# One core, a state-space mixer and a sparse FFN: base rows moved to VectorE, packed attention, and an earlier token choice

## What is computed

```python
h  = layernorm(x) * (1 + ca) + sa
x  = x + ga * mixer(h)            # x, z projections, causal conv, silu, B, C, dt, state scan,
                                  # group norm, gate by silu(z), output projection
h  = layernorm(x) * (1 + cb) + sb
x  = x + gb * ffn(h)

def ffn(h):
    weights = h @ router_w + router_b
    idx     = sorted indices of the 127 largest weights      # of 1024 tokens
    xs      = h[idx]
    q, k, v = heads(rmsnorm(xs) @ wq, wk, wv)                # 16 heads of 16, rope on q and k
    a       = softmax(q @ k.T / 4 + mask[idx, idx])
    x1      = xs + (a @ v) @ wo
    x2      = x1 + gelu(rmsnorm(x1) @ w1) @ w2
    out     = 0; out[idx] = x2 * weights[idx]
    return out + h * (1 - (weights > threshold))
```

## Time and profile before

| what | value |
|---|---|
| runs | 1646.09, 1646.8, 1646.9 us; median 1646.8 |
| profiled execution | 1651.24 us |
| its span | 1649.5 us, 23125 instructions |
| mean granted TensorE clock | 0.942 of 2.4 GHz |
| busy: VectorE | 990.2 us (60%) |
| busy: ScalarE | 688.7 us (42%) |
| busy: GpSimd | 482.9 us (29%) |
| chain that ended last | TensorE 76%, VectorE 11%, issue 4%, ScalarE 3%, DMA 2%, GpSimd 2% |

### The profile page before, as it was taken

How to read it: one execution, slowest core, us unless ns; L and a number is a source line. 1 busy time by engine, 2 the same in 40 slices (tenths; PEclk the granted TensorE clock), 3 DMA queues, 4 the chain that set the end, 5 groups by cost and what they waited for, 6 DMA issues and landing times.

```text
span 1649.5 us, 23125 instructions
## 1 busy us (share of the span) xinstructions
PE 1455.1 (88%) x8673; PEld 931.3 (56%) x8736; DVE 990.2 (60%) x2632; ACT 688.7 (42%) x1345; POOL 482.9 (29%) x505
## 2 busy tenths in 40 slices
PE   7999989989799897999989997998979989897445
PEld 2447545765467654675447654675546754466434
DVE  2337675368735695376763787356862669537661
ACT  4443533436244452635435362444516354252221
POOL 3014231322505323133313325043231432323240
PEclk9999999999999999999999999899999999999666
DMA  8000000100102000020000101020010200001010
GB/s 274 1 1 27 26 29 13 43 27 26 42 1 69 7 33 29 1 69 26 28 15 26 44 26 42 0 68 1 32 36 1 69 20 20 29 4 40 26 42 4
DMA packets 47534, 54.25 MB, mean 33 GB/s; under 512 B 7608, under 2 KB 42296, under 8 KB 47424
## 3 DMA queue, kind: packets, MB, share of 16 engines
q1 hardware_dynamic: 41408, 46.42, 8.6%
q0 software_dynamic: 6016, 6.35, 1.5%
HBM read 34.84 MB, written 17.87 MB: 32 GB/s over the span
## 4 chain that ended last, share of the span: by engine, by line
PE 76%; DVE 11%; issue 4%; ACT 3%; DMA 2%; POOL 2%; POOLq 0%; DVEq 0%; SPq 0%
PE ps L1515 36%; PE ps L1679 7%; PE ps L1630 4%; PE ps L1589 3%; PE ps L1582 3%; DMA Mt<-mask,midx 2%; PE ps L1642 2%; PE ps L1601 2%; PE ps L1816 2%; PE ps L1826 2%; DVE xT L1199 2%; PE ps L1794 2%; PE ps L1616 2%; PE ps L1620 1%; PE ps L1607 1%
## 5 line engine op out<-in xcount | busy, mean ns | idle before, releaser
L1515 PE MATMUL ps<-xT,wc_s 128*128 128x512 f32 x512 | 235.8, 608 | 0.0
L1515 PE MATMUL ps<-xT,wb_s 128*128 128x512 f32 x512 | 235.1, 608 | 0.1
L1022 DVE SCALAR_TENSOR_TENSOR xT<-xc,cols_s,xT 128x512 f32<-128x512 f32 x192 | 168.4, 923 | 3.2 <-ACT xT L713 0.6
L1515 PEld LDWEIGHTS ps<-xT,wb_s 128*128 128x128 f32 x512 | 97.2, 196 | 115.4 <-issue 107.8
L1515 PEld LDWEIGHTS ps<-xT,wc_s 128*128 128x128 f32 x512 | 97.9, 196 | 109.5 <-issue 109.2
L587 POOL TENSOR_TENSOR EC<-EC,CT 128x512 f32<-128x512 f32 x64 | 92.0, 1437 | 152.2 <-DVE Mt L1264 149.7
L1679 PE MATMUL ps<-CT,xT 128*128 128x256 f32 x512 | 115.1, 386 | 16.3 <-DVE xT L1199 16.3
L1679 PEld LDWEIGHTS ps<-CT,xT 128*128 128x128 f32 x512 | 98.6, 194 | 35.5 <-issue 21.9
L1515 PE MATMUL ps<-hT,wx_s 128*128 128x512 f32 x256 | 116.5, 610 | 2.3 <-ACT hT L677 2.3
L611 POOL TENSOR_TENSOR sm<-sm,mhalf 128x1 f32<-128x1 f32 x24 | 14.5, 603 | 354.7 <-DVE sm L1400 324.8
L1515 PE MATMUL ps<-hT,wz_s 128*128 128x512 f32 x256 | 112.3, 592 | 0.0
(11 more groups left out here) (296 smaller groups left out, 2770.0 us busy)
## 6 DMA issues: line engine op xcount, KB each, us to landing
BT<-x SPq DMA_DIRECT2D x8, 1024.0 KB, 6.5
xr<-x SPq DMA_DIRECT2D x8, 1024.0 KB, 7.6
x_scratch<-xr SPq DMA_DIRECT2D x32, 256.0 KB, 2.1
out<-EC SPq DMA_DIRECT2D x32, 256.0 KB, 2.1
modrow<-mod_scratch SPq DMA_DIRECT2D x8, 512.0 KB, 4.4
w_s<-w SPq DMA_DIRECT2D x2, 1024.0 KB, 12.0
xT<-wmod SPq DMA_DIRECT2D x1, 1024.0 KB, 8.4
wb_s<-wbT SPq DMA_DIRECT2D x1, 1024.0 KB, 11.0
```

The lines of the kernel that those rows point to most:

```text
L1022: ins = v.scalar_tensor_tensor(dst, xcv[:, m, half * HALF + tap:half * HALF + tap + HALF], cols_s[:, m, tap:tap + 1], dst, ALU.mult, ALU.add)
L1515: ins = t_.matmul(bank[:, :], w[:, k, m * P:(m + 1) * P], rhs[:, k, half * HALF:(half + 1) * HALF], start=k == 0, stop=k == nk - 1)
```

## The change

- **Layer norm.** Jobs of the ring are renumbered so that the two x tiles (half 0, m = 0 and 1) come between the two halves of the transposes. ScalarE's copies of half 0 (`ln_rows(b, 0)`) move ahead of `ln_apply` of half 1, into the scan before.
- **Rank and index sum** move on TensorE from behind B/C tiles five and seven to behind tiles three and four.
- **Base rows** are made by VectorE: piece 0 between `ffn_pick` and `ffn_norm`, pieces 1 to 3 between `decay_steps` and `ffn_scores`. Each piece has a store semaphore of its own, and group r of the scores waits for store r alone.
- **Scores.** The same 16 matmuls, but neighbours in the order belong to different r, so to different row groups and banks.
- **Scaling.** The probabilities are divided by their sums ahead of the transposes (`ffn_probs` on VectorE, four groups); the transposes wait for it (`pn_ready`). `ffn_o` is gone.
- **AV.** v is the weight: `vz` holds for each head 32 columns, of which 16 are v and 16 are zero, and AT (128 columns) streams. Four neighbours write to different groups of 32 PSUM partitions; an even and an odd head are accumulated into one group. The result is oT itself, so that the transposes of o (job F_OT) go, and ScalarE copies AV's bank. GpSimd zeroes vz once a batch behind the gathers; ScalarE's copy of v becomes two.

```diff
@@ GpSimd
-            def base(b, j):
-                q = slice(2 * j, 2 * j + 2)
-                pool.wait_ge(hn2_ready, at(hn2_ready, b, 2 * j + 2))
-                for i, row in enumerate((cg, sg)):
-                    chO(pool, b, g.tensor_tensor(h2[:, q, :], h2[:, q, :],
-                                                 row.unsqueeze(1).broadcast_to([P, 2, D]),
-                                                 ALU.add if i else ALU.mult))
-                g.tensor_tensor(h2[:, q, :], h2[:, q, :], xr[:, q, :], ALU.add).then_inc(base_ready, 1)
...
                 g.memset(qkr[:, :, :, HD:2 * HD], 0.0).then_inc(qkz_ready, 1)
+                g.memset(vz[:, :, :], 0.0).then_inc(vz_ready, 1)
...
             def ffn_first(b):
-                pool.wait_ge(G_ready, at(G_ready, b, T))
-                base(b, 0)
-                base(b, 1)
                 gather(b)
                 small_pow(b, fv_ready, fr_ready, 0)
                 small_pow(b, fs_ready, frr_ready, 2)
-                base(b, 2)
-                base(b, 3)
-                chO.end()
                 small_pow(b, fs2_ready, frr2_ready, 4)
@@ ScalarE
                 if not last:
                     ln_apply(b + 1, 0)
+                    ln_rows(b + 1, 0)
                     ln_apply(b + 1, 1)
...
-                ln_in(b)
-                x_copies(b, ((0, (0, 1, 2, 3)), (1, (0,))))
+                x_copies(b, ((0, (0, 1)),))
+                ln_rows(b, 1)
+                x_copies(b, ((0, (2, 3)), (1, (0,))))
@@ VectorE
+            def base(b, j):
+                q = slice(2 * j, 2 * j + 2)
+                dve.wait_ge(hn2_ready, at(hn2_ready, b, 2 * j + 2))
+                for row, op in ((cg, ALU.mult), (sg, ALU.add)):
+                    chR(dve, b, v.tensor_tensor(h2[:, q, :], h2[:, q, :],
+                                                row.unsqueeze(1).broadcast_to([P, 2, D]), op))
+                v.tensor_tensor(h2[:, q, :], h2[:, q, :], xr[:, q, :], ALU.add).then_inc(base_ready, 1)
...
-                dve.wait_ge(base_stored, at(base_stored, b, 64))
                 for r in range(4):
                     q, h = F_SC + r, slice(4 * r, 4 * r + 4)
                     dve.wait_ge(*ffn.full(b, q))
+                    dve.wait_ge(base_stored[r], at(base_stored[r], b, 16))
...
+            def ffn_probs(b):
+                for r in range(4):
+                    h = slice(4 * r, 4 * r + 4)
+                    dve.wait_ge(prob_ready, at(prob_ready, b, 4 * r + 4))
+                    chR(dve, b, v.reciprocal(den[:, h], den[:, h]))
+                    v.tensor_tensor(scr[:, h, 0:NSEL], scr[:, h, 0:NSEL],
+                                    den[:, h].unsqueeze(2).broadcast_to([P, 4, NSEL]), ALU.mult
+                                    ).then_inc(pn_ready, 1)
...
                     ffn_pick(f)
+                    base(f, 0)
                     ffn_norm(f)
...
                 decay_steps(b)
                 if f is not None:
+                    for j in range(1, 4):
+                        base(f, j)
                     ffn_scores(f)
                 decay_parts(b)
                 if f is not None:
-                    ffn_o(f)
+                    ffn_probs(f)
@@ TensorE
-                    for m in range(4):
+                for m in range(4):
+                    for r in range(4):
+                        q = slice(32 * r, 32 * r + 32)
                         ins = t_.matmul(ffn.bank(F_SC + r)[:, m * P:m * P + NSEL], qT[q, m, :], kT[q, m, 0:NSEL],
                                         start=True, stop=True)
...
-                    pe.wait_ge(prob_ready, at(prob_ready, b, 4 * r + 4))
+                    pe.wait_ge(pn_ready, at(pn_ready, b, r + 1))
...
-                    for m in range(4):
-                        o = (4 * m + r) * HD
-                        ins = t_.matmul(bank[:, o:o + HD], AT[0:NSEL, 4 * r + m, :], vs[0:NSEL, o:o + HD],
-                                        start=True, stop=True)
+                for k in range(KD):
+                    for e in range(2):
+                        for i in range(4):
+                            h = 8 * k + 2 * i + e
+                            ins = t_.matmul(bank[32 * i:32 * i + 32, k * P:(k + 1) * P], vz[0:NSEL, h, :],
+                                            AT[0:NSEL, 4 * (h % 4) + h // 4, :], start=e == 0, stop=e == 1)
...
                 ln_in(b, 0)
                 if f is not None:
                     output(f, T - 1)
-                ln_in(b, 1)
                 if f is None:
                     pe.wait_ge(wload, 16 * len(first_loads))
-                x_proj(b, 0, range(3))
+                x_proj(b, 0, (0, 1))
+                ln_in(b, 1)
+                x_proj(b, 0, (2,))
...
-                bc_proj(b, 0, (0, 1, 2, 3, 4))
+                bc_proj(b, 0, (0, 1, 2))
                 if f is not None:
                     ffn_rank(f)
-                bc_proj(b, 0, (5, 6))
+                bc_proj(b, 0, (3,))
                 if f is not None:
                     ffn_idx(f)
-                bc_proj(b, 0, (7,))
+                bc_proj(b, 0, (4, 5, 6, 7))
...
                 decay_rows(b)
                 if f is not None:
-                    pe.wait_ge(*ffn.read(f, F_AV))
-                    ffn_turn(f, F_OT, ob)
+                    ffn_wo(f)
                 bc_proj(b, 1, (6,))
-                if f is not None:
-                    ffn_wo(f)
                 bc_proj(b, 1, (7,))
```

More of the change, by code:

```diff
@@ L710, in last_tap @@
                 for m in range(KC):
-                    act.wait_ge(*proj.read(b, J_X + half * KC + m))
+                    act.wait_ge(*proj.read(b, J_X[half][m]))
                     o = TAPS - 1 + half * HALF
@@ L843, in ffn_oT @@
             def ffn_oT(b):
-                act.wait_ge(*ffn.full(b, F_OT))
-                bank = ffn.bank(F_OT)
-                ins = a.activation(oT_, bank[:, 0:D], ACT.Copy)
-                ins.then_inc(ffn.drained[F_OT % 4], 1)
+                act.wait_ge(*ffn.full(b, F_AV))
+                a.activation(oT_, ffn.bank(F_AV)[:, 0:D], ACT.Copy).then_inc(ffn.drained[F_AV % 4], 1)
             def ffn_hnbT(b):
@@ L920, in _ @@
             ln_apply(0, 0)
+            ln_rows(0, 0)
             ln_apply(0, 1)
@@ L1500, in ln_in @@
                 for k in range(KD):
-                    q = J_H + half * KD + k
+                    q = J_H[half][k]
+                    if q >= 4:
+                        pe.wait_ge(*proj.read(b, q - 4))
                     for i in range(4):
@@ L1519, in x_proj @@
             def x_proj(b, half, ms):
-                pe.wait_ge(*proj.read(b, J_H + (2 * half + 2) - 1))
+                pe.wait_ge(*proj.read(b, J_H[half][1]))
                 for m in ms:
-                    project(b, J_X + half * KC + m, wx_s, m, hT, KD, half)
+                    project(b, J_X[half][m], wx_s, m, hT, KD, half)
             def z_proj(b, half, ms):
```

78 lines of the change are left out of this document (35 added, 43 removed).

## The result

Four runs of the changed kernel took 1538.87 to 1547.94 us, median **1541.9**; four of the kernel before, median 1646.85. The ratio is 0.9348, with an interval of 0.9322 to 0.9374: 6.5% faster (the two medians alone divide to 0.936). The forecast range ended at 1540: the median lies 2 us inside it, and 1646.85 us times the ratio, 1539.5, just outside. So the range hardly held. The profiled execution, the slowest of the four, took 1547.94 us (span 1546.2, mean granted clock 0.959 after 0.942), 103.3 less than the one of before. The sum of the forecast, 77.5, is to be held against this 103.3.

A forecast was written before the change was run, and what follows sets the result against it. TensorE, busy 88% of the span, was taken to set the end. Terms -19 -43 -15.4 -12 -10.5 -17 -1.6 +37 +12 -8 sum to -77.5 us, from 1646.8 to 1569 us; range 1540 to 1602.

The forecast's parts named there:

- transposes of o and the scaling: Behind AV: the transpose of o and VectorE's scaling there go, -1.6 us in all.
- Layer norm: Two x projections of half 0 fill TensorE's second wait, and slow transposes quicken: -19 us, bounds -8 and -24.
- Gap ahead of `hn`: TensorE's 6.30 us wait for VectorE's `hn`, behind the dt projection, goes in each batch but the tail: -43 us.
- dt rows and the clock behind the gap: TensorE's wait for VectorE's dt rows goes, -15.4 us; half-rate clock behind the idling ahead of `hn` goes, -12 us.
- Base rows on VectorE at no cost: VectorE's 12 base operations lie in its waits for the gathered row and the scores: costed at nothing, uncovered 8.7 us a batch.
- Scores, new wait and its clock: Packed scores -10.5 us; transposes of probabilities wait for VectorE's scaling, +37 (bounds +3, +7 a batch); its clock +12 (0 to 20).
- AV: 32-column weights in four column groups take 1.2 us instead of 3.64: -2.4 us a batch, -17 us.
- Tail: Last FFN pass, alone: one-hots -5.0, base rows net 0 up to the scores, AV, scaling and transpose -3.3; together -8 us.
- The first, packing gives next to nothing: Attention matmuls: weights or row pieces serialise, AV stays 3.5 us, scores 2.2: +22 us, 1591 us; chance 0.09.
- The second, a gap partly closed: Ahead of `hn`: mask or index come 5.5 us late, 3 us of wait and the clock cost stay: +33, 1602 us; chance 0.08.
- The third, no new wait: At the probabilities' transposes: decay parts and scaling fit into TensorE's two tiles, -49, 1520 us; chance 0.05.
- The fourth, late stores: Scores wait for base row stores; slower than before if landing exceeds 17 us, 1667 us at 20; chance 0.02.

The follow-up runs named there:

- u_rank: Changed kernel with rank and index sum back at their old places in TensorE's order, base rows staying on VectorE: 1595.6 us, 0.9651 of the kernel before.
- u_av: Changed kernel with AV in its old form (AT as weight, 16 columns of v streaming) and the transposes of o: 1578.3 us, 0.9562 of the kernel before.
- u_base: Changed kernel with base rows back on GpSimd at their old places, rank and index sum staying forward: 1604.8 us, 0.9723 of the kernel before.
- m_probs: Changed kernel with VectorE's scaling of the probabilities ahead of the decay parts instead of behind them: 1513.0 us, 0.9174 of the kernel before.
- u_scores: Changed kernel with the scores issued bank by bank again: 1533.7 us, 0.9268 of the kernel before.
- m_stats: Changed kernel with scaling before decay parts, one more B/C tile before the probabilities' transposes, next x's statistics a scan step earlier: 1486.8 us, 0.8981 of the kernel before.

## Where the forecast held, and where it failed

The waits came out as forecast, nearly every one; what failed is TensorE's clock. The step that failed outright is the term for the transposes of o and the scaling (-1.6 us): it put the clock behind the old AV at nothing, and the runs show 8.0 us there. Next to it the clock behind the new wait was mis-sized: 12 us taken, 6.6 measured. The terms one by one:

**Layer norm** (-19): -18.5, and that it is so close is in part luck. The waits gave 15.8 us (35.1 to 19.3) and not 18.4, since eight first waits stay and not seven; the rest is the rate of the transposes. And the stage took 20.42 us in this execution but 19.16 in `u_rank`, by which the term would be -27, outside its own bounds. **Gap ahead of `hn`** (-43): -43.7, with the times to spare about as counted (0.84 and 2.9 us; 0.6 and 2.5 were forecast). **dt rows and the clock behind the gap** (-27.4): -31.6. The rows' wait was right; of the clock I had 1.7 us a batch, and 2.3 were there. `u_rank`, where VectorE is free and the gap is back, has 6.98 us in that stage against 4.58 without the gap. So 2.4 us are the slow clock behind 6.2 us of idling.

**Base rows on VectorE at no cost**: right. VectorE waits 2.06 us for the scores, and the stage from decay sums to scores is 4.80 us in all kernels.

**Scores, new wait and its clock** (-10.5 +37 +12 = +38.5): +30.8. The mechanism held, and the terms add up to 7.7 too much. Score matmuls took 1.17 us (1.3 forecast). VectorE began 1.25 us behind their start (1.8), the scalings came at a distance of 0.80 (0.95), and the tile behind took 4.54 us instead of 3.6, a clock cost of 0.9 instead of 1.7. First wait 3.06 us, where 3.6 was forecast. (The forecast's 0.064 and 0.055 us a record are 0.068 and 0.060 by its rows, 1.09/16 and 1.93/32; nothing hangs on that.)

**AV** (-17): -18.8. 32 records take about 1.0 us, 1.2 was taken.

**Transposes of o and scaling** (-1.6): -9.6, and this is the step that failed. The transposes took 0.23 us a batch, 1.6 in all, as forecast. But the forecast had no term for the clock behind the old AV, though the kernel before shows it in the windows over its AV and what follows:

```profile
1060.00:1065.00 5.00, 5.00 (x38) 4.76 (x37) 0.05 (x1) 0.60 (x1) 0.00 (x0) 0.78 0.00 0
1065.00:1070.00 5.00, 5.00 (x22) 3.21 (x20) 1.20 (x3) 2.99 (x4) 0.00 (x0) 0.54 0.00 0
```

TensorE is busy for all of these 10 us, and yet the granted clock is 0.78 and then 0.54: mostly the lower level, 1.2 of 2.4 GHz. The same stretch after, behind the packed AV:

```profile
998.00:1003.00 5.00, 5.00 (x58) 3.22 (x58) 0.82 (x2) 1.79 (x3) 0.00 (x0) 1.00 0.00 0
```

From decay rows to carry rows the old kernel took 9.28 us in two batches, 9.29 in one and 10.97 to 12.06 in the other four, those in which the clock fell behind AV; the new one takes 8.91 in all seven. `u_av` shows it by itself: with the old AV back, 1.39 us a batch are lost behind it, with no wait in the 7 us before it. I had looked for the clock only behind idle time, and the old AV has none. 8.0 us of the 25.9 that were missed (103.4 - 77.5) lie here.

**Tail** (-8): -12.0. The one-hots gave their 5.0. "Net 0" for the base rows held: up to the scores 3.1 us were gained, and as much was lost behind them, where VectorE starts its scores later (11.39 us from scores to transposes, 8.33 in `u_base`, whose base rows are on GpSimd). The rest is clock. From AV to wo are 1.67 us, where the forecast makes 3.2 (8.69 less 4.25 and 1.2): AV ran at the full clock, 1.08 us and not 2.6:

```profile
1512.27 3.75 PE L1790 MATMUL ps<-ident,EC 128*127 128x128 f32 x16 [10.22 <-DVE EC L1386]
1516.80 1.08 PE L1803 MATMUL ps<-EC,ftmp 127*32 127x128 f32 x32 [0.78 <-ACT EC L832]
```

Another 1.0 us came from wo on and 1.4 in the group norm. The 1.4 are chance: up to the rank the tail took 31.2 us here and 31.0 in `u_rank`, but 32.6 in `m_probs`, with the same work.

In sum the missed time is 7.7 at the new wait, 8.0 behind AV, 4.2 behind the `hn` gap, 4.0 in the tail, 1.8 in AV and 0.7 at the gap itself, less 0.5 in layer norm. Some 20 of it are TensorE's clock: 8.0 behind AV, 4 to 5 behind the gap, 5.4 behind the new wait (12 was taken, 0.94 x 7 was there), 4 in the tail. These stand on the same side, which is why bounds added up as independent gave a range at whose edge the result lies.

**The rivals.** The first, packing gives next to nothing because the records serialise, is excluded by the two rows of 1.17 and 1.08 us (the scores' gain in time is nothing all the same, but for another reason, see `u_scores`). The second, a gap partly closed, is excluded in size: the mask came 7.1 us behind the indices instead of 6.5, a cost of 0.6 us and within the time to spare. The third, no new wait, was wrong for this kernel and right for `m_probs`, whose 29 us are what I should have named as the worth of an order. The fourth, late stores, does not show: VectorE's first operation on the scores is released by TensorE, and a base row store takes 2.1 us on the page, the same as in the earlier trace rows.

## What to carry to other kernels

Count both engines from the one point where they meet; that gave the new wait to half a microsecond, and would have shown at once that a step which another engine needs (the scaling) must not stand behind work that nobody waits for yet (the decay parts). A chain with long transfers in it starts where the engine that feeds it issues the feeding step: two moved calls of a microsecond or two each decided some 50 us. Look at the granted clock behind every stretch of odd work, not only behind idle time, and pack a matmul only if what reads it is not itself the bound.

## What was not expected of the hardware

- The clock fell with TensorE never idle, behind 3.6 us of full-width weight loads with 16 streamed columns each (0.78 and 0.54 of full speed in the windows above): in four of seven batches of the kernel before and in all seven of `u_av`. It stayed full behind the same product with 32-column weights and 128 streamed columns. Whether the wide loads or the short streams do it, no run separates.
- Small packed matmuls are fast. AV's 32 records of 127 rows and 32 columns, in four column groups, take 1.08 us, 0.034 each, though a weight load alone is 110 ns. So the loads must overlap each other and the running matmuls (least, median and longest of them behind the count):

```profile
L1803 PEld LDWEIGHTS ps<-EC,ftmp x256: 106/110/110, 276.1 to 1517.5; 127*32 127x32 f32 x128
```

  The Trainium skill, page "TensorE: Matmul & The Clock Gate", Part 3, The mechanism, lets weight loads overlap running matmuls only when the row group differs. All of these share every row and differ by column group alone; the trace disagrees, and the measurement decides.
- The gain of a removed wait depends on a clock that varies from one execution to the next. Behind the 2.38 us wait of layer norm the stage took 19.2 us in some batches and 20.5 to 20.8 in others: one of seven short in the changed kernel's profile, three of seven in that of `u_scores`, all in that of `u_rank`. That is up to 9 us a run, the size of the spread of these kernels. With the wait gone (`m_stats`) the stage was 19.7, so the wait does not set this alone. What does is open.
- VectorE and GpSimd slow each other. VectorE's six conv passes took 9.11 us beside the base rows and 4.31 alone; GpSimd's base operations took 1.69 us each beside them, where the median of their 64 records is 1.28. It is not only operations with several inputs: the one-hots, which read one tile and a column of scalars, took 6.70 us beside the base rows in the tail and 1.66 alone.
